# Layer 1 rows of a pair stage: read from a per-batch copy in SBUF and PSUM, or from where the first stage left the projection

## The reference, cut to what matters

```python
x = layernorm(L0_attn_x)                        # 16 batches, 256 tokens, 256 features, float32
xn = layernorm(x) * gamma + beta
h = einsum('bsd,fd->bsf', xn, W1)               # 128 features f
pair = relu(h[:, :, None, :] - h[:, None, :, :] + b1)      # every pair i, j of the 256 tokens
pair = relu(einsum('bijf,gf->bijg', pair, W2) + b2)        # 64 features g
sim = einsum('bijg,og->bijo', pair, W3)[..., 0] + b3       # 256 x 256 for each batch, diagonal 0
top_idx = top_k(sim, 25)                        # each token attends to 25 others, 32 heads
...
out = x + attention(xn, top_idx) + shared_mlp(x) + routed_experts(x)   # 8 experts, 2 a token
```

## Time and profile before

| what | value |
|---|---|
| median of 3 runs | 1795.44 us (1788.97 to 1803.44) |
| the profiled execution | 1796.21 us |
| its span | 1794.5 us |
| TensorE busy | 1670.4 us, 93% |
| VectorE busy | 1523.4 us, 85% |
| ScalarE busy | 1442.2 us, 80% |
| GpSimd busy | 1123.8 us, 63% |
| mean granted TensorE clock | 0.989 |

### The profile page before, as it was taken

The page is one execution under the profiler, slowest core; times in us unless marked ns, Lnnn a source line. Parts: engine busy times, 40 slices in busy tenths (PEclk is TensorE's granted clock), DMA queues, the critical chain, the costliest instruction groups (busy, mean ns, idle before and its releaser), DMA issues.

```text
span 1794.5 us, 30234 instructions
## 1 busy us (share of the span) xinstructions
PE 1670.4 (93%) x9092; PEld 722.9 (40%) x9092; DVE 1523.4 (85%) x4205; ACT 1442.2 (80%) x2787; POOL 1123.8 (63%) x1027
## 2 busy tenths in 40 slices
PE   7999979899998999899999999899999999999998
PEld 6732212222222222222222222222222499997887
DVE  6899958879888998989988999888998688866888
ACT  5699868989888989989998999899998877843342
POOL 3207776766676777767666677777675644455556
PEclk9999989999999999999999999999999999999999
DMA  5722111111111111111111111111221166632333
GB/s 184 249 85 83 55 50 41 42 44 45 45 47 42 48 46 46 49 44 49 43 49 44 46 48 45 47 45 49 66 66 37 51 193 206 184 122 77 118 118 106
DMA packets 80071, 136.85 MB, mean 76 GB/s; under 512 B 22336, under 2 KB 46528, under 8 KB 79936
## 3 DMA queue, kind: packets, MB, share of 16 engines
q0 software_dynamic: 31744, 69.27, 14.2%
q1 hardware_dynamic: 48192, 65.91, 11.2%
HBM read 95.24 MB, written 39.85 MB: 75 GB/s over the span
## 4 chain that ended last, share of the span: by engine, by line
ACT 41%; PE 30%; issue 9%; DVE 7%; another core or an unknown queue 5%; DMA 1%; SPq 1%; POOL 1%; POOLq 0%; DVEq 0%; ACTq 0%
ACT arena L1094 22%; PE ps L905 18%; ACT arena L1139 17%; PE ps L945 7%; PE ps L917 4%; DVE arena L1336 3%; PE ps L962 1%; ACT arena L1143 0%; DMA arena<-xn_rows 0%; DVE idx L1467 0%; POOL arena L815 0%; DVE top L1460 0%; DVE arena L1510 0%; DVE arena L1710 0%
## 5 line engine op out<-in xcount | busy, mean ns | idle before, releaser
L734 POOL DMA_INDIRECT arena<-kv_rows,gidx x800 | 892.7, 1116 | 454.1 <-issue 227.9
L905 PE MATMUL ps<-arena,w2t 128*64 128x512 f32 x4096 | 986.2, 604 | 88.0 <-ACT arena L1139 46.0
L1139 ACT ACTIVATE arena<-ps,b 128x1024 f32<-128x1024 f32 x512 | 630.5, 1233 | 141.3 <-remote 91.2
L905 PEld LDWEIGHTS ps<-arena,w2t 128*64 128x64 f32 x4096 | 282.6, 137 | 784.0 <-issue 668.2
L1336 DVE TENSOR_SCALAR arena<-h_now 128x256 f32<-128x256 f32 x1184 | 382.7, 379 | 79.1 <-remote 46.8
L1336 DVE TENSOR_SCALAR arena<-arena 128x256 f32<-128x256 f32 x1184 | 380.7, 378 | 58.7 <-remote 31.0
L1094 ACT ACTIVATE arena<-ps,h_now 128x256 f32<-128x256 f32 x864 | 377.0, 611 | 0.0
L1094 ACT ACTIVATE arena<-ps,arena 128x256 f32<-128x256 f32 x756 | 328.2, 605 | 0.0
L917 PE MATMUL ps<-arena,w3win 128*32 128x512 f32 x2048 | 278.5, 612 | 1.8 <-issue 1.8
L917 PEld LDWEIGHTS ps<-arena,w3win 128*32 128x32 f32 x2048 | 41.0, 108 | 212.0 <-issue 152.6
L1510 DVE TENSOR_TENSOR arena<-arena 128x1152 f32<-128x1152 f32 (+4 forms) x160 | 100.3, 627 | 0.4
(11 more groups left out here) (158 smaller groups left out, 2111.6 us busy)
## 6 DMA issues: line engine op xcount, KB each, us to landing
arena<-kv_rows,gidx POOLq DMA_INDIRECT x800
slot_inputs<-arena SPq DMA_DIRECT2D x16, 640.0 KB, 4.0
arena<-slot_inputs SPq DMA_DIRECT2D x40, 256.0 KB
slot_outputs<-arena SPq DMA_DIRECT2D x40, 256.0 KB
arena<-in_L_attn_x_dram SPq DMA_DIRECT2D x16, 256.0 KB, 3.1
xn_rows<-arena SPq DMA_DIRECT2D x16, 256.0 KB, 3.9
arena<-in_L_attn_x_dram SPq DMA_DIRECT2D x8, 512.0 KB
arena<-xn_rows SPq DMA_DIRECT2D x8, 512.0 KB
```

The costliest lines, as they stand in the source:

```text
L734: pool.indirect_dma_start(out=kvg[:, h, r, :], out_offset=None, in_=kv_dram, in_offset=bass.IndirectOffsetOnAxis(ap=gidx[:, h, r:r + 1], a ...
L905: last = nc.tensor.matmul(ps_l2(n)[v * G2:(v + 1) * G2, u, :], w2t[:, :], r1[:, n % R1, 4 * u + 2 * v:4 * u + 2 * v + 2, :], start=True, s ...
L1139: nc.scalar.activation(r2[:, n % R2, :].rearrange("p (u n) -> p u n", u=2), ps_l2(n), ACT.Relu, bias=b2[:, 0:1]).then_inc(r2_done, 1)
```

## The change

Both engines' rows read `h_both` at the batch's columns, in SBUF. The copies for batches 0 to 14 go, the moves into PSUM go, and so do the second buffer and bank 7's use for it. Only batch 15 is copied, at step 17 of batch 14, into `h_last`, and its rows read that. Where `batch_copied` and `batch_moved` were waited for, ScalarE now waits once for the first stage's own write (`h_saved`, before its very first row), and both engines wait for `last_copied` before batch 15. SyncE's loads over `h_both` wait for `last_copied` and until both engines have finished their rows of batch 14.

```diff
-        h_now = [part(2 * S, 2), sb("h_now1", [P, 2, S])[:, :, :]]
-        hneg_now, hb_now = ([h[:, k:k + 1, :].rearrange("p o n -> p (o n)") for h in h_now] for k in range(2))
+        h_last = part(2 * S, 2)
...
-        ps_hneg = [ps[:, 7, i * S:(i + 1) * S] for i in range(2)]
...
+        def h_rows(b, k):
+
+            h = h_both[:, k:k + 1, b * S:(b + 1) * S] if b < NB - 1 else h_last[:, k:k + 1, :]
+            return h.rearrange("p o n -> p (o n)")
...
-            sp.wait_ge(batch_copied, NB)
+            sp.wait_ge(last_copied, 1)
+            sp.wait_ge(r1_dve, (NB - 1) * BSTEPS)
+            sp.wait_ge(r1_act, (NB - 1) * BSTEPS)
...
-            def relu1(b, i, s, first):
+            def relu1(b, s):
                 n = b * BSTEPS + s
                 if n >= R1:
 
                     act.wait_ge(l2_done, n - R1 + 1)
-                if s == 0:
-
-                    act.wait_ge(batch_copied, b + 1)
-                    if not first:
-                        act.wait_ge(batch_moved, b)
+                if n == 0:
+
+                    act.wait_ge(h_saved, START + 2)
+                if b == NB - 1 and s == 0:
+                    act.wait_ge(last_copied, 1)
                 for k in range(dve_rows(s), STEP_ROWS):
                     at = step_rows(s)[k]
-                    last = nc.scalar.activation(r1[:, n % R1, k, :], hneg_now[i] if first else ps_hneg[i], ACT.Relu,
-                                                bias=hb_now[i][:, at:at + 1])
+                    last = nc.scalar.activation(r1[:, n % R1, k, :], h_rows(b, 0), ACT.Relu, bias=h_rows(b, 1)[:, at:at + 1])
...
-            def move_next(b, i, first):
-
-                act.wait_ge(batch_copied, b + 2)
-                if first:
-                    act.wait_ge(route_done, 1)
-                nc.scalar.activation(ps_hneg[1 - i], hneg_now[1 - i], ACT.Copy).then_inc(batch_moved, 1)
-
...
-                    if s == MOVE and b < NB - 1:
-                        move_next(b, b % 2, b == 0)
...
-            def copy_batch(b, i):
-
-                nc.vector.tensor_copy(h_now[i], h_both[:, :, ds(b * S, S)]).then_inc(batch_copied, 1)
+            def copy_last():
+
+                nc.vector.tensor_copy(h_last, h_both[:, :, (NB - 1) * S:NB * S]).then_inc(last_copied, 1)
...
-                row = nc.vector.tensor_scalar(r1[:, (b * BSTEPS + s) % R1, k, :], hneg_now[i], hb_now[i][:, at:at + 1], 0.0, ALU.add, ALU.max)
+                row = nc.vector.tensor_scalar(r1[:, (b * BSTEPS + s) % R1, k, :], h_rows(b, 0), h_rows(b, 1)[:, at:at + 1], 0.0, ALU.add, ALU.max)
...
                 dve.wait_ge(h_saved, START + 2)
-                copy_batch(0, 0)
-                dve.wait_ge(batch_copied, 1)
...
-                            if s == COPY and done < 3:
-                                copy_batch(b + 1, 1 - i)
+                            if s == COPY and b == NB - 2:
+                                copy_last()
```

More of the change, by code:

```diff
@@ L342, in lsn_attention_moe_block @@
         l3_done = sem("l3_done")
-        batch_copied = sem("batch_copied")
-        batch_moved = sem("batch_moved")
+        last_copied = sem("last_copied")
         sim_taken = sem("sim_taken")
@@ L414, in lsn_attention_moe_block @@
         GROUPS = BSTEPS // 2
-        COPY, MOVE = 17, 20
+        COPY = 17
         def dve_rows(s):
             return (6, 7, 6, 3, 3, 7, 5, 4, 5, 2, 7, 6, 2, 2, 3, 6)[s % STEPS]
+        def h_rows(b, k):
+            h = h_both[:, k:k + 1, b * S:(b + 1) * S] if b < NB - 1 else h_last[:, k:k + 1, :]
+            return h.rearrange("p o n -> p (o n)")
         passed = {name: sem(f"{name}_passed") for name in ("dve", "pe", "pool")}
@@ L1106, in keep_second @@
                 for s in range(ahead):
-                    relu1(0, 0, s, True)
+                    relu1(0, s)
                 act.wait_ge(h_ready, b + 1)
@@ L1148, in _ @@
                     if n >= ROWS_AHEAD:
-                        relu1(b, b % 2, s, b == 0)
-                    if s == MOVE and b < NB - 1:
-                        move_next(b, b % 2, b == 0)
+                        relu1(b, s)
                     if n == 9:
@@ L1332, in relu1_begin, with relu1_row @@
                     dve.wait_ge(l2_done, n - R1 + 1)
-            def relu1_row(b, i, s, k):
+            def relu1_row(b, s, k):
                 at = step_rows(s)[k]
-                row = nc.vector.tensor_scalar(r1[:, (b * BSTEPS + s) % R1, k, :], hneg_now[i], hb_now[i][:, at:at + 1], 0.0, ALU.add, ALU.max)
+                row = nc.vector.tensor_scalar(r1[:, (b * BSTEPS + s) % R1, k, :], h_rows(b, 0), h_rows(b, 1)[:, at:at + 1], 0.0, ALU.add, ALU.max)
                 if k == dve_rows(s) - 1:
@@ L1342, in rows_ahead @@
                 dve.wait_ge(h_saved, START + 2)
-                copy_batch(0, 0)
-                dve.wait_ge(batch_copied, 1)
                 for s in range(ROWS_AHEAD):
                     for k in range(dve_rows(s)):
-                        relu1_row(0, 0, s, k)
+                        relu1_row(0, s, k)
             dve.wait_ge(x_loaded, 16)
@@ L1522, in _, with pair_batch @@
             TAKE, TOP = 5, 6
-            def pair_batch(b, i, done):
-                dve.wait_ge(batch_copied, b + 1)
+            def pair_batch(b, done):
+                if b == NB - 1:
+                    dve.wait_ge(last_copied, 1)
                 for s in range(0 if done else ROWS_AHEAD, BSTEPS):
@@ L1537, in pair_batch @@
                     for k in range(dve_rows(s)):
-                        relu1_row(b, i, s, k)
+                        relu1_row(b, s, k)
                         if k == 0:
-                            if s == COPY and done < 3:
-                                copy_batch(b + 1, 1 - i)
+                            if s == COPY and b == NB - 2:
+                                copy_last()
                             if topk and s == TAKE:
@@ L1577, in pair_batch @@
                                 scale(summed)
-            pair_batch(0, 0, 0)
-            pair_batch(1, 1, 1)
+            pair_batch(0, 0)
+            pair_batch(1, 1)
             for b in range(2, NB - 1):
-                pair_batch(b, b % 2, 2)
-            pair_batch(NB - 1, 1, 3)
+                pair_batch(b, 2)
+            pair_batch(NB - 1, 3)
             def split_low(parts, high_done, done, low_done):
```

## The result

The changed kernel takes 1820.5 us (median of 4 runs, 1812.0 to 1826.9), the kernel before 1793.0 in the same set (4 runs, 1789.0 to 1803.4). The ratio is 1.0113, with a 95% interval from 1.0061 to 1.0165; the medians are 27.5 us apart. The profiled execution took 1821.0 us against 1796.2, so 24.8 us more. Nearly all of it lies in the pair stage: its last `relu2` starts at 1440.1 us, where it started at 1417.0, 23 us later. Every ratio here is taken without the runs that lie over 1.5% above the fastest of their kernel, which on two of the later chips is more than half of the runs of the kernel before; there a ratio can be a per cent away from that of the medians, and both are given.

The account below looks back on a forecast made before the run. In the pair stage three engines are near full, with ScalarE's rows the chain's largest item. Terms 33.7 + 5 - 2.6 - 0.4 - 0.4 = +35 us on the profiled 1796.2 gave 1831.5, against the median 1831; range 1809 to 1852.

Parts of the forecast that it names:

- What decides: Pair stage: a ScalarE row reading SBUF instead of PSUM takes 0.398 to 0.400 us, not 0.365, so 0.034 more.
- Rival (b): ScalarE's rows: the 34 ns is a mark of batch 0, not the source; not slower, 1787 us; chance 0.06.
- The size: Whole kernel: all terms together add 35 us to the profiled execution's 1796.2, giving 1831.5 us.
- ScalarE's rows on the path: Pair stage: 990 of the 1620 rows that change source lie on the chain, at 0.034 us each, +33.7 us.
- rival (a): Pair stage: rows cost more, but ScalarE's idle time takes up half the price; about 1812 us; chance 0.15.
- Two signs that the prediction named: Pair stage's chain in the changed profile: ScalarE's share rises and TensorE's falls; no size given.
- sum for a pair of steps: Pair stage, two steps: TensorE needs 4.58 us, ScalarE 4.46; SBUF rows add 0.23, making ScalarE the bound by 0.11.
- Rows off the path: Pair stage: 630 ScalarE rows off the chain use up its slack beside TensorE; +5 us, bounds 0 and 21.
- The moves: ScalarE's 15 moves into PSUM, 0.28 us each, go: -2.6 us, bounds 0 and 4.2.
- The copies: VectorE's 16 copies become one: -0.4 us inside the pair stage, bounds 0 and -4.6, and -0.4 at its start.
- The late loads: SyncE's loads over `h_both` start 40 and 12 us later, still 83 us before first use: 0, bound +6 us.
- Rival (c): Pair stage: all 1620 rows count, 1848 us; TensorE idles more and its clock may fall, 1855; chance 0.09.

Follow-up runs that it names:

- the pair with pauses: Changed kernel, VectorE also waiting for its own last row at five steps of 16, against the kernel before with the same waits: 1804.5 and 1795.5 us.

## Why the prediction was right

**What decides** was right. ScalarE's rows went from 0.365 to 0.399 us (six in 2.39), the value taken from batch 0. The experiment with only their source gave the whole change's time to 0.3 us. Rival (b), that the 34 ns belong to batch 0, is out. The 400 ns by the rule in the Trainium skill ("ScalarE: Activation LUTs", What ACT_TABLE_LOAD costs), which knows no difference by source, fit these rows and not those from PSUM. The other one ("Perfetto Trace Analysis", Optimizing Scalar/DVE Operations), 93 against 51 ns, has the right sign; the rows say 34 and not 42.

**The size** was too large: +35 us forecast for the profiled execution, +24.8 measured, +27.5 by the medians and 1.0113 x 1793 - 1793 = +20 by the ratio, which starts at 1.0061, 11 us. The term that was mis-sized is "ScalarE's rows on the path", +33.7. I priced every row on the chain in full and argued against rival (a) that ScalarE "can't work off what it hasn't been given" in TensorE's pauses. The traces say otherwise: its waits in them fell from 98 to 74 us, and from 94 to 64 in the pair with pauses, while TensorE's own idle time without a cause didn't shrink (32 to 43). The account of ScalarE's order (51 more work, 25 less waiting) gives 26 in place of the sum's 35. Rival (a) was thus half right, as a part of the forecast and not as a case beside it, though its remark that the waits for layer 2 can shrink was not: they went from 41 to 40. (Half of the price gone is 1796 + 18 = 1814, and not the 1812 stated there.) Two signs that the prediction named came out the other way with it: ScalarE's share of the chain didn't rise, and TensorE's didn't fall. How the pauses are taken up wasn't measured by itself. The likely course, argued only: while ScalarE is the later of the two, TensorE has done all that it may before it pauses, and the pause costs ScalarE less.

Without those pauses the price depends on what it is held against. The changed kernel's 1704.2 stands 10 us over the median of the kernel before on its chip and 37 over its quickest run (1667.5), 14 and 26 over the same two of the kernel with everything but the source, and 23 over the 1681.3 of the kernel before with VectorE's pauses, on another chip. The prediction's own sum for a pair of steps fits the undisturbed case: there TensorE with 4.58 us is the bound, ScalarE goes from 4.46 to 4.69, and 240 pairs x 0.11 = 26 us, an estimate from the earlier trace rows. So here too a part of the 51 us went into waits, this time those for layer 2: 41 us in everything but the source, 19 in the changed kernel, 22 less.

**Rows off the path** (+5) can't be told apart from the first term. **The moves** were taken at 0.28 us each; no run shows their gain by itself, but a copy of their size stands at 0.28 on the chain of the experiment with added copies. **The copies** brought nothing that can be told (4 us by the median, the interval of the ratio from 0.9992 to 1.0105), as the bounds of 0 and -5 said. At the start the first rows of VectorE came at 92.81 where they had come at 93.43, 0.6 us for the 0.4 taken.

**The late loads** cost nothing, as forecast, in the trace and alone. But one row was read wrongly: the gather held for 5.85 us was put down to the slot loads ahead of it. In the changed kernel the same gather is held before any load is issued, and on other chips gathers are held far from any load, under long runs of VectorE. The bound of +6 for it did no harm.

**Rival (c)**, a lower clock because TensorE idles more, had it backwards on the chips without TensorE's pauses: 0.993 to 0.996 in the changed kernel's runs, 0.985 to 0.994 in those of the kernel before beside it. On the first chip it was a little lower in the changed kernel, 0.986 against 0.989 in the two profiled executions. In the stretches shown it fell with one long idle stretch (0.59 above, 0.90 in the earlier trace rows), and not with many short gaps (1.00 in batch 0).

## What to carry to other kernels

Compare two sources of an instruction by the distance of back-to-back instructions on the chain and not by the mean in flight: here the mean fell from 608 to 513 ns while the rate got worse by 34 ns, and with 1620 instructions on the bounding engine that is the whole result. A copy of 0.28 us that moves an operand read over a hundred times to the memory that the engine reads faster can pay for itself many times. In a pipeline of three nearly full engines price a longer order by what the engine does and what it waits: part of the added time goes into waits that are there anyway, here half of 51 us in the main pair. Once ScalarE was the bound, nine tenths of the next 54 us showed.

## What the runs showed of the hardware

Two of five submissions differ from the others in something that the trace doesn't name: ScalarE waits some thirty times, for up to 15 us, for a TensorE that pauses or slows down with nothing to wait for, and the same kernel takes 1793 to 1801 us in place of 1686 to 1701. Each submission had its own chip, so the chip is the likely cause, but no chip was tried twice.

A gather of GpSimd can be held while VectorE issues without a gap, up to 12.45 us in place of 0.95. In the trace read for it no held gather went on for more than 0.3 us behind a pause of VectorE, but seven of eleven ended without one. With five short waits of VectorE in 16 steps none took over 4.1 us on one chip and 2.5 on the other. The Trainium skill ("Perfetto Trace Analysis", Optimizing Scalar/DVE Operations) says that GpSimd and VectorE share a read port of SBUF, which a VectorE instruction using both holds as a lock. The traces fit that but don't show the port; that the hold can last over 30 instructions is theirs. Why it strikes only some gathers, and what ends it without a pause, is open.
